# TensorE's loop in the scan stage: eight chunks per pass in place of two, with the last fourteen chunks written out

## What is computed

```python
def step(s, inp):
    q_, w_, k_, v_, a_, b_ = inp
    sa = einsum('bhij,bhj->bhi', s, a_)
    s = s * w_[:, :, None, :] + sa[..., None] * b_[:, :, None, :] + v_[..., None] * k_[:, :, None, :]
    return (s, einsum('bhij,bhj->bhi', s, q_))
_, y = jax.lax.scan(step, s0, (qt, wt, kt, vt, at, bt))
```

## Time and profile before

| | before |
|---|---|
| median of 3 runs | 4864.01 us |
| the profiled execution's own time | 4857.42 us |
| its span, first to last instruction | 4855.6 us |
| mean granted TensorE clock | 0.959 of full speed |
| TensorE matmul busy | 4353.1 us (90%) |
| TensorE weight load busy | 3654.0 us (75%) |
| VectorE busy | 3336.5 us (69%) |
| ScalarE busy | 2938.6 us (61%) |
| GpSimd busy | 2292.0 us (47%) |
| fetches of instructions | 188 packets (queue q14) and 71 packets (queue q8) |

### The profile page before, as it was taken

The page is one execution under the profiler, slowest core; times in us unless marked ns, Lnnn a source line. Parts: engine busy times, 40 slices in busy tenths (PEclk is TensorE's granted clock), DMA queues, the critical chain, the costliest instruction groups (busy, mean ns, idle before and its releaser), DMA issues. The chain is left out here.

```text
span 4855.6 us, 281580 instructions
## 1 busy us (share of the span) xinstructions
PE 4353.1 (90%) x114072; PEld 3654.0 (75%) x114072; DVE 3336.5 (69%) x10277; ACT 2938.6 (61%) x8550; POOL 2292.0 (47%) x3196
## 2 busy tenths in 40 slices
PE   7888888778888888764999999999999999999998
PEld 6888888668888888653677777777777777777776
DVE  4666666568888888464666666666666777777775
ACT  4777777634444444343666666666666666666665
POOL 1222222157777777402454455544455555555553
PEclk8999999879999999887999999999999999999999
DMA  3333333467777777596667666667676666677765
GB/s 88 87 93 95 95 91 93 96 152 162 165 166 165 166 164 166 132 280 195 153 160 159 155 155 155 161 159 158 157 190 164 161 159 161 168 167 164 164 160 123
DMA packets 1454099, 728.62 MB, mean 150 GB/s; under 512 B 676624, under 2 KB 1398288, under 8 KB 1452816
## 3 DMA queue, kind: packets, MB, share of 16 engines
q1 hardware_dynamic: 1402448, 652.89, 58.1%
q10 hardware_dynamic: 51392, 73.02, 5.0%
HBM read 410.48 MB, written 315.15 MB: 149 GB/s over the span
## 5 line engine op out<-in xcount | busy, mean ns | idle before, releaser
L2354 ACT ACTIVATE l_prob<-l_prob,l_nb,l_rq 128x160 f32<-128x160 f32 x1024 | 522.3, 511 | 201.2 <-DVE l_nb L2189 200.8
L2015 POOL TENSOR_TENSOR l_k<-l_kn,l_tab 128x512 f32<-128x512 f32 x128 | 162.7, 1271 | 613.0 <-DVE l_kn L2163 613.0
L2031 POOL TENSOR_TENSOR l_prob<-l_prob,l_rinv 128x320 f32<-128x320 f32 x512 | 362.7, 719 | 53.5 <-DVE l_rinv L2171 53.3
L2560 PE MATMUL lD<-l_hid,w 128*128 128x128 f32 x3072 | 363.9, 275 | 0.0
L2560 PEld LDWEIGHTS lD<-l_hid,w 128*128 128x128 f32 x3072 | 353.3, 192 | 0.0
L2552 PEld LDWEIGHTS lA<-l_hn,w 128*128 128x128 f32 x2048 | 242.8, 195 | 110.3 <-POOL l_hn L2049 61.0
L2198 DVE STREAM_TRANSPOSE l_pb<-l_prob 128x320 f32<-128x320 f32 x512 | 250.5, 498 | 104.2 <-POOL l_prob L2031 104.2
L2025 POOL TENSOR_TENSOR l_qr<-l_q 128x512 f32<-128x512 f32 x128 | 162.5, 1269 | 329.2 <-DVE l_q L2127 329.2
L1097 POOL TENSOR_TENSOR sc_aqx<-sc_late,sc_headmask 128x256 f32<-128x256 f32 x256 | 175.4, 685 | 275.5 <-PE sc_Y L1190 274.0
L1173 PE MATMUL sc_AB<-sc_aq,sc_bkx 32*32 32x32 f32 x16384 | 256.5, 198 | 38.5 <-POOL sc_bkx L1097 28.2
L497 POOL TENSOR_TENSOR rk<-rk,bkraw 128x256 f32<-128x256 f32 x64 | 54.6, 871 | 478.0 <-DVE bkraw L383 478.0
(11 more groups left out here) (273 smaller groups left out, 13069.5 us busy)
## 6 DMA issues: line engine op xcount, KB each, us to landing
l_pT<-scratch_pz SPq DMA_DIRECT2D x1024, 128.0 KB, 3.8
scratch_pz<-l_pb SPq DMA_DIRECT2D x256, 320.0 KB, 3.0
scratch_qkz<-l_qk SPq DMA_DIRECT2D x128, 512.0 KB, 2.9
l_qkT<-scratch_qkz SPq DMA_DIRECT2D x512, 128.0 KB, 3.2
scratch_cm<-cm SPq DMA_DIRECT2D x64, 512.0 KB, 4.1
sc_early<-scratch_cm ACTq DMA_DIRECT2D x59, 512.0 KB, 4.5
scratch_tok<-vt SPq DMA_DIRECT2D x512, 48.0 KB, 1.8
scratch_part<-sc_att SPq DMA_DIRECT2D x64, 384.0 KB
```

The source lines that it names most:

```text
L2015: tt(k1[s][:], kn[s][:], wide(2, slice(0, DH)), ALU.mult)
L2031: tt(prob[s][:, pair], prob[s][:, pair], rinv[s][:, pair].unsqueeze(2).broadcast_to([P, 2, SPAN]), ALU.mult).then_inc(Q["pn"][s].sem, 1)
L2354: last_ = nc.scalar.activation(prob[s][:, h], prob[s][:, h], ACT.Exp, scale=rq8[s][:, h:h + 1], bias=nb[s][:, h:h + 1], accum_out=sums[s][ ...
L2560: last_ = mm(bank[s][3][:, c * P:(c + 1) * P], w2[:, m, c * P:(c + 1) * P], hid[s][:, m], start=(c == 0 and m == 0), stop=(c == CC - 1 and ...
```

## The change

The loop body of line 1240 holds eight chunks, and the loop runs (64 - 4) * 4 / 8 = 30 passes. The loop of line 1243 is gone: its fourteen chunks are written out one after the other. The last two chunks stay written out. The same matmuls run in the same order, with the same waits on the same counts.

```diff
-    LEAD = 4
+    LEAD, BODY = 4, 2 * UC
...
-                with pe.Fori(0, (NU - LEAD) * UC // 2) as i:
-                    for c in range(2):
-                        chunk(2 * i + c, c, True, True)
-                with pe.Fori((NU - LEAD) * UC // 2, NU * UC // 2 - 1) as i:
-                    for c in range(2):
-                        chunk(2 * i + c, c, False, True)
+                with pe.Fori(0, (NU - LEAD) * UC // BODY) as i:
+                    for c in range(BODY):
+                        chunk(BODY * i + c, c % 2, True, True)
+                for n in range((NU - LEAD) * UC, NU * UC - 2):
+                    chunk(n, n % 2, False, True)
                 for c in range(2):
                     chunk(NU * UC - 2 + c, c, False, c == 0)
```

## The result

The changed kernel takes 6502.97 us (median of 4 runs, 6499.48 to 6510.88) against 4863.66 us before. The ratio is 1.3375, with a 95% interval of 1.3351 to 1.3398. It is 1639 us slower. The forecast was 6410 us, and the range 6090 to 6730 us holds the result.

A forecast was written before the change was run, and what follows sets the result against it. TensorE sets the pace, and the longer code must be fetched block by block: 4857.4 + 1490 (main loop) + 53 (written-out end) = 6400 us, 6410 us on the median's scale, range 6090 to 6730 us.

The forecast's parts named there:

- Reading the stops as fetches: TensorE's scan-stage first passes: stops of 1.43 to 1.85 us every 256 instructions are waits for 16 KB code blocks.
- The body doesn't stay: Main loop: eight chunks, 5184 instructions or 21 to 22 blocks, are fetched anew in every pass.
- Main loop: Scan stage: thirty passes of 81.8 us, 2454 us against 963.8 us, 1490 us more.
- The term of a block: TensorE in the scan stage: each missing block of 256 instructions takes 3.8 us, range 3.4 to 4.2 us.
- The back edge: End of each main-loop pass: the branch to a missing block costs 2 us beyond that block's own period.
- Written-out end: Fourteen chunks after the main loop: 28.3 blocks at 3.8 us, 107.5 us against 54.4 us, 53 us more.
- The clock: TensorE in the scan stage: falls to the lower level, costs nothing; 256 instructions there take 1.9 us, under 3.8.
- The other engines' programs: Engines besides TensorE: programs unchanged, nothing queues behind a new wait, no cost added.
- The 97 back edges: Main and short loops: fewer back edges at 0.41 us each save at most 40 us, if nothing else slows the loop.
- Part of the body stays: Rival, main loop: six blocks stay and 15 are fetched per pass, 5940 us in all; chance 0.04.
- The whole body stays: Rival, main loop: no fetches after the first pass, 4920 us in all; chance 0.06.
- Fetched ahead in time: Rival, scan stage: blocks arrive within 1.56 us, no stops, back edges saved, 4825 us in all; chance 0.03.

The follow-up runs named there:

- 1646: Kernel before with four chunks per main-loop pass, first product, most of the second, Y's value part and three quarters of the last Y product left out: 4857.49 us.
- 1838 instructions: Kernel before with four chunks per main-loop pass, first product, all but one matmul of the second and Y's value part left out: 5912.69 us.
- 1726 instructions: Kernel before with four chunks per main-loop pass, less work as in the seven-block body, but six matmuls kept in the second product: 5485.01 us.
- the shifted local loops: Kernel before with 136 semaphore increments behind the scan stage's last chunk, moving the local stage's loops within their blocks: 4989.99 us, ratio 1.0258.

## Why the prediction was right

**Reading the stops as fetches.** Right. They were identified by their even distance of 256 instructions and by the queue. Every run changed stops and fetches together.

**The body doesn't stay.** Right. No row of before had the capacity; the nearest bodies that stay have 1577 recorded matmuls and weight loads. The runs place the limit for the main loop between 1646 and 1838 instructions from where it starts. The Trainium skill (Advanced Engine Details and Errata, ISA Cache) gives TensorE 128 KB in lines of 16 KB, which makes eight blocks; the runs agree, if the block fetched ahead counts as one of the eight. The same list says "Only 2 cache lines!", and there the runs differ: bodies that touch 4 to 7 blocks ran without a fetch.

**Main loop.** 2545.6 us came for 2454, 92 us too low, and this is the larger miss. The term of a block was taken as 3.80 us from seven distances and measured 4.01 us over the 19 of a pass: 21 * 0.21 = 4.4 us per pass. The back edge was taken as 2 us beyond its block and was 85.2 - 21 * 4.01 = 1.0 us, so 1.0 us less. 30 * 3.4 = 102 us would be the difference; the first pass took 2545.6 - 29 * 85.19 = 75.1 us, 10 us less than a later one, which leaves 92 us. The later stretches of before, with 3.91 to 4.31 us, were nearer than the first pass, 3.32 to 3.57 us. Why these differ isn't settled: the DMA share was 0.56, 0.21 and 0.02 in the quick ones, and 0.09 in the last two chunks, which were slow, so the load of the DMA engines doesn't explain it.

**Written-out end.** 114.6 us for 107.5, the same term: 114.6 / 28.3 = 4.05 us per block. The median of the kernel with this edit alone gives 57.6 us more, the forecast 53.

**The other terms.** The clock fell to 0.50, and nothing shows that it cost time of its own, as expected: matmul busy time of 1192.84 us is under half of the 2545.60 us. But this is argued: of the first pass of before, one distance at a clock of 0.89 was 3.32 us and two at 0.50 were 3.57 and 3.52 us, too few to tell. The other engines' programs didn't matter: TensorE waited for none of them in the stage. The 97 back edges, at most 40 us, were swallowed; the run with an added one (0.51 us with all that came with it) doesn't speak against that bound.

**The rivals.** "Part of the body stays" falls with 22 fetches in every pass. No run shows it: near the limit, with 1726 instructions and in the shifted local loops, whole passes fetch and whole passes don't. "The whole body stays" falls. "Fetched ahead in time" falls with 1418 us of stops. The rule of the Trainium skill (Runtime: NRT & Kernel Launch, Instruction fetch mechanics) that fetching is hidden behind a sequencer that reads slowly holds in the local stage at 12.5 us per block, but for the target of a back edge (the stop of 5.3 us above), and fails in the scan stage, where 256 instructions are run in 1.56 us.

## What to carry to other kernels

Before a loop body is made longer on TensorE, the only engine tried here, count its instructions (a float32 matmul counts four here) in blocks of 256: seven blocks ran free, while eight (with 144 instructions in the eighth) or more were fetched anew in every pass, at about 4 us per block where one is run in 1.56 us, to save 0.4 us per back edge. Where an engine is through a block in less than about 4 us, straight code pays too, so short code that is run often beats long code. When a stage that nobody touched becomes slower or scatters, look at the instruction queue: the change may have moved its loop across a block's edge.

## What had not been expected

136 instructions that do nothing, put ahead of a stage that isn't changed, cost 129 us in the median of four runs (4989.99 against 4860.51 us), and 96 cost 3 us. A loop at the limit may fetch all of its blocks in one pass and none in the next. And leaving out 29% of TensorE's instructions in the main loop (920 for 1296) made the whole kernel slower, 4951.61 against 4861.74 us in one run each, with 115 more blocks fetched in another stage; the shift of the code without any work left out did the same.
